# Attention and feed-forward layer on one core: spread from 32 rows, scores in three fp32r passes, GpSimd's output sums moved

## The chip, the cores and the metric

One core of one Trainium2 chip. The metric is the device time of the one launch, in microseconds. Three runs of the kernel before gave 348.83, 346.28 and 348.46; the median is 348.46.

## The reference

The input is x (4 rows of 1024 positions, 256 values), a context of 64 positions per row, and an integer mask over the context. LN is layer normalisation without weights.

```python
def attention(q_in, ctx, mask):               # 16 heads of 16; k and v have one head, shared
    q, k, v = q_in @ Wq + bq, ctx @ Wk + bk, ctx @ Wv + bv
    scores = einsum('bhqd,bkd->bhqk', q, k) / 4
    p = softmax(where(mask == 0, -1e9, scores))
    return einsum('bhqk,bkd->bhqd', p, v) @ Wo + bo

def ffn(x):                                   # 9 paths 256 -> 64 -> 256; one path for each position
    xm = mix[0] * left(x) + mix[1] * x + mix[2] * right(x)
    path = argmax(tanh(xm @ Wo1 + bo1) @ Wo2 + bo2)
    return LN(x + ((xm @ W1[path] + b1[path]) @ W2[path] + b2[path])) * gamma + beta

x = x + attention(LN(x), ctx, mask)
x = x + ffn(LN(x))
```

## The kernel before

**Chunks and steps.** Work is cut into 8 chunks of 512 positions: chunk (b, j) is half j of row b. A chunk has NT = 4 tiles of 128 positions; the model width 256 is KD = 2 blocks. Each engine (TensorE, ACT, VectorE, GpSimd, and SP for DMAs) has its own program, written out by hand, and semaphores join them. All five go through the same steps. A step has a chunk n in attention (softmax, P V, projection, LN 2), the next one, `front`, whose q and maxima are made, the one after, `after`, whose LN 1 is done, and an earlier one, f, in the FFN. For n = (r, 0) the FFN works on f = (r-1, 0), for n = (r, 1) on (r-1, 1). Steps: (0,0) and (0,1) without an FFN part, (1,0) to (3,0) full, (3,1) without a `front`, then a tail with the FFN of (3,0) and (3,1). The step shown in most rows, from 191.34 us, has n = (2,1), front (3,0), f (1,1).

**Precision.** Most large products are made in fp32r, with each operand split into a rounded high part and a remainder (hi, lo): hi*hi, hi*lo, lo*hi are three passes into one PSUM bank. W1, W2 and Wq are done so. The scores for the softmax are plain fp32, which the trace shows as two records for each matmul.

**Softmax.** `scores_for_max` makes approximate scores (position on the partitions) from the rounded q (`qr`) and the keys `kmx`; VectorE's `take_max` reduces them, and the maxima, split in two bf16 parts and transposed, are subtracted inside PSUM. `scores_transposed(t)` makes the real scores with the keys on the partitions: for each of four row quarters g of q a product of 32 rows of `kst` with 32 rows of q into bank 2+g (L556), then the mask (L559) and the maxima (L563). There are two calls, t = 0 and 1, in each step. ACT does the exponential, `pv` makes P V into banks 0 and 1 (L575) and the denominators (L581).

**Normalising the attention.** `invert` on VectorE takes the reciprocals of the denominators (L1169) and splits them in a rounded part and a remainder in different rows (L1172, L1174). `spread` on TensorE (L589) copies them to all rows with 8 products of `bc` (128 rows, ones where row and column belong together) and `rDs` into banks 4 and 5. ACT copies P V to `osb` (L872), VectorE multiplies the two (`attn_normalise`, L1180), TensorE projects with Wo (`project_out`, L599) into banks 0 and 1.

**FFN.** PSUM banks 6 and 7 are given in turn to the uses in the order of the list `uses`: h0, h4, h1, gate, h2, h3, rep0, rep1, ... `w1(m)` makes a hidden block, `gate` the path scores, VectorE's `argmax` (L1246 to L1263) turns them to a one-hot `oh`, `rep(m)` (L663) spreads it over the hidden rows, `select(m)` (L1270) keeps the chosen path, ACT rounds (`selected_hi`, L928), GpSimd makes the remainder (`selected_lo`, L1511), `w2_tiles` (L681, L682, L686) multiplies, VectorE adds the residual and applies LN 3.

**Mixing.** `second_mix` and `early_mix` on VectorE (L1207, L1209, L1212; two halves c = 0, 1) make the neighbour sum of a later FFN chunk, ACT rounds it, GpSimd makes the remainders (L1487, L1493).

**GpSimd's order in a step before.** Key operands `kmx`, `kst` (for a new row), `rstd1`, mix remainders, `value_operand` (`vd`, waits for the denominators), `add_beta` (L1480), `add_bo` (L1474), five `selected_lo`, `rstd2` (L1454, then L1467, for LN 2, which ACT applies at L892, after which TensorE transposes xh2 at L608), `rstd` of LN 3, and `finish` (L1500: times gamma; L1505: plus the residual with beta). `finish` waits for LN 3, so it runs at the beginning of the next step. SP loads the next x when `add_bo` has read the old one.

## Time and profile before

| what | value |
| --- | --- |
| median of 3 runs | 348.46 us (346.28 to 348.83) |
| profiled execution | 348.3 us, span 346.5 us |
| TensorE (PE) busy | 311.3 us, 90% of the span |
| VectorE (DVE) busy | 287.4 us, 83% |
| GpSimd (POOL) busy | 189.4 us, 55% |
| ACT busy | 177.5 us, 51% |
| mean granted clock of TensorE | 0.983 |

The span is the time from the first to the last instruction of the profiled execution; 1.8 us of its time lie around it. In the rows a number after x counts instructions that were merged into one line, the second column is the time from the first one's start to the last one's end. The shape before `f32<-` is what is written, the one behind it what is read; `128*64` before a matmul's shapes is rows and columns of the array that it uses. An fp32 matmul has two records. PEclk 1.00 means 2.4 GHz.

### The profile page before, as it was taken

The numbers are of one execution on the slowest core, as the hardware profiler recorded it, in microseconds if no ns is written. First come the engines' busy times: TensorE is split into PE (matmuls) and PEld (weight loads), VectorE is DVE, ScalarE is ACT, GpSimd is POOL, SyncE is SP. The second block draws the span as 40 slices with busy tenths as digits, with TensorE's granted clock in tenths as the row PEclk, the third lists the DMA queues.
The fourth block names the chain that finished last, engine by engine and source line by source line (L and its number), as shares of the span: only waits on it lengthen the run. The fifth ranks groups of instructions, "written<-read, shape, count | busy, mean of one in ns | idle before, by whom it ended". The sixth has DMA issues, their size and how long they took to land.

```text
span 346.5 us, 6989 instructions
## 1 busy us (share of the span) xinstructions
PE 311.3 (90%) x2700; PEld 230.7 (67%) x2700; DVE 287.4 (83%) x616; ACT 177.5 (51%) x275; POOL 189.4 (55%) x226
## 2 busy tenths in 40 slices
PE   1688889789999999999999999999999999799980
PEld 1573464556679657876779577966787578667980
DVE  2776898998789898989898998988797967689866
ACT  1354725626743676268644784377425753267400
POOL 0263202671584399628882699528962976173043
PEclk9999899999999999999999999999999999899997
DMA  7852200020020010200120010001000010001003
GB/s 225 239 117 72 78 0 3 0 77 3 2 78 0 2 61 2 78 1 8 58 76 2 1 62 2 0 3 51 11 2 1 3 62 0 0 2 61 3 0 121
DMA packets 20570, 13.53 MB, mean 39 GB/s; under 512 B 10097, under 2 KB 20282, under 8 KB 20538
## 3 DMA queue, kind: packets, MB, share of 16 engines
q1 hardware_dynamic: 18898, 12.53, 12.2%
q10 hardware_dynamic: 1640, 0.57, 0.7%
q8 instruction: 21, 0.34, 0.4%
q14 instruction: 11, 0.09, 0.1%
HBM read 8.90 MB, written 4.19 MB: 38 GB/s over the span
## 4 chain that ended last, share of the span: by engine, by line
PE 76%; DVE 14%; ACT 4%; issue 2%; DMA 2%; POOL 1%; DVEq 0%; SPq 0%; ACTq 0%; POOLq 0%
PE ps L433 16%; PE ps L438 7%; PE ps L599 7%; PE ps L681 6%; PE ps L686 5%; PE ps L682 5%; PE ps L556 5%; PE ps L581 4%; PE ps L575 4%; DVE osb L1180 3%; PE ps L663 2%; PE ps L648 2%; PE ps L559 2%; PE ps L492 2%; DVE st L1103 2%
## 5 line engine op out<-in xcount | busy, mean ns | idle before, releaser
L1454 POOL TENSOR_TENSOR rs<-ve,halfneg 128x4 f32<-128x4 f32 x24 | 26.9, 1120 | 98.0 <-DVE ve L1119 98.0
L867 ACT ACTIVATE e<-ps 128x1024 f32<-128x1024 f32 x32 | 31.1, 1024 | 16.6 <-PE ps L563 16.6
L1156 DVE TENSOR_REDUCE mx<-ps 128x16 f32<-128x1024 f32 x32 | 38.0, 1214 | 0.3 <-PE ps L531 0.3
L681 PE MATMUL ps<-w2h,hmh 128*128 128x256 f32 (+1 forms) x140 | 35.6, 289 | 0.0
L682 PE MATMUL ps<-w2l,hmh 128*128 128x256 f32 (+1 forms) x140 | 34.7, 283 | 0.0
L1511 POOL TENSOR_TENSOR hml<-hs,hmh 128x512 fp32r<-128x512 f32 x24 | 30.2, 1272 | 7.8 <-ACT hmh L928 7.7
L599 PE MATMUL ps<-wo,osb 128*128 128x256 f32 x128 | 31.3, 390 | 2.0 <-DVE osb L1180 2.0
L1500 POOL TENSOR_TENSOR y<-xh2f,gms 128x256 f32<-128x256 f32 x28 | 22.2, 824 | 17.4 <-DVE xh2f L1128 17.4
L918 ACT ACTIVATE hs<-ps,b1s 128x512 f32<-128x512 f32 x28 | 19.3, 690 | 22.6 <-PE ps L438 22.5
L433 PE MATMUL ps<-xmh,w1h 128*128 128x512 f32 x80 | 27.7, 428 | 3.0 <-DVE xmh L1231 2.2
L892 ACT ACTIVATE xh<-x,vb,rs 128x256 f32<-128x256 f32 x24 | 12.5, 591 | 32.4 <-POOL vb L1467 32.4
L928 ACT ACTIVATE hmh<-hs 128x512 fp32r<-128x512 f32 x28 | 17.4, 627 | 20.2 <-DVE hs L1270 20.2
L599 PEld LDWEIGHTS ps<-wo,osb 128*128 128x128 f32 x128 | 23.2, 190 | 6.3 <-issue 2.5
L681 PEld LDWEIGHTS ps<-w2h,hmh 128*128 128x128 f32 (+1 forms) x140 | 26.5, 189 | 0.8
L682 PEld LDWEIGHTS ps<-w2l,hmh 128*128 128x128 f32 (+1 forms) x140 | 26.4, 189 | 0.0
L438 PE MATMUL ps<-xml,w1h 128*128 128x512 f32 x80 | 26.0, 407 | 0.0
L433 PE MATMUL ps<-xmh,w1l 128*128 128x512 f32 x80 | 25.6, 401 | 0.0
L1505 POOL TENSOR_TENSOR y<-y,x1b 128x256 f32<-128x256 f32 x28 | 24.4, 899 | 0.6
L1270 DVE TENSOR_TENSOR hs<-hs,ps 128x512 f32<-128x512 f32 x28 | 18.5, 680 | 7.3 <-PE ps L663 7.3
L1474 POOL TENSOR_TENSOR x<-xin,bos 128x256 f32<-128x256 f32 x32 | 23.9, 778 | 0.8
L686 PE MATMUL ps<-w2h,hml 128*128 128x256 f32 (+1 forms) x140 | 21.4, 282 | 0.3 <-POOL hml L1511 0.3
L556 PE MATMUL ps<-q,kst 32*128 32x512 f32 x128 | 19.1, 640 | 1.2 <-ACT e L867 1.2
(163 smaller groups left out, 791.8 us busy)
## 6 DMA issues: line engine op xcount, KB each, us to landing
xin<-in_x SPq DMA_DIRECT2D x8, 512.0 KB, 3.7
out<-y SPq DMA_DIRECT2D x7, 512.0 KB, 2.9
min_<-in_mask_Bx1xSxS_ik SPq DMA_DIRECT2D x8, 128.0 KB, 4.2
hs<-in_L_ffn_W SPq DMA_DIRECT2D x2, 288.0 KB
y<-in_constants SPq DMA_DIRECT2D x1, 512.0 KB, 10.1
hs<-in_L_ffn_W SPq DMA_DIRECT2D x1, 512.0 KB
out<-xin SPq DMA_DIRECT2D x2, 256.0 KB, 2.2
cst<-in_constants SPq DMA_DIRECT2D x1, 384.0 KB, 6.7
```

The source lines that it names most:

```text
L433: nc.tensor.matmul(out_, lhs[i](k), rhs(k), start=(i == 0 and k == 0), stop=False)
L438: mm = nc.tensor.matmul(out_, lhs(k), rhs(k), start=False, stop=(k == KD - 1))
L556: nc.tensor.matmul(ps[:, 2 + g, :], kst[quarter(g), :], q[quarter(g), t, :], start=True, stop=False)
L599: mm = nc.tensor.matmul(ps[:, k // 2, (k % 2) * D:(k % 2 + 1) * D], osb[:, c, k * P:(k + 1) * P], wo[:, c, :], start=(c == 0), stop=(c == ...
L681: nc.tensor.matmul(o, L.hi(m, r)[:, ks], w2h[0:r, m, :], start=(m == 0), stop=False)
L682: nc.tensor.matmul(o, L.hi(m, r)[:, ks], w2l[0:r, m, :], start=False, stop=False)
L686: mm = nc.tensor.matmul(o, L.lo(m, r)[:, ks], w2h[0:r, m, :], start=False, stop=(m == NM - 1))
L867: nc.scalar.activation(e[:, 2 * i:2 * i + 2, :], ps[:, bank:bank + 2, :], ACT.Exp).then_inc(s_e, 1)
L1156: v.tensor_reduce(mx[:, k, :].rearrange("p (a h) -> p a h", a=2), ps[:, bank:bank + 2, :].rearrange("p a (h s) -> p a h s", s=SK), AX.X, A ...
L1454: g.tensor_tensor(ln[7][:, :], ln[6][:, :], halfneg[:, :], ALU.pow).then_inc(s_r, 1)
L1505: a = g.tensor_tensor(y[:, k], y[:, k], x1b[:, j, k], ALU.add)
L1511: g.tensor_tensor(usual.lo(m, r), usual.selected(m, r), usual.hi(m, r).bitcast(F32), ALU.subtract).then_inc(s_hl, 1)
```

## The change

- **Spread.** The constant `bc` holds for each 32 rows what it held for 128: KD * P columns instead of KD * NT * P. `spread` takes for tile k only the 32 rows (row quarter k) that hold its reciprocals, and writes bank `SPREAD_BANKS[k]` = 0, 1, 4, 5. So it waits for the P V copy as well. `attn_normalise` is two instructions of two tiles each, and `project_out` waits for its own half.
- **First mask behind P V.** rep(0), the first block of the path mask, is made by TensorE right behind `pv`, ahead of w1(2) and w1(3); the order of the two banks changes with it. VectorE's `select(0)` stands ahead of `invert`. The tail keeps the old order by a class of its own (`behind`).
- **Scores.** ACT's q copy writes the rounded q (`qr`) itself. VectorE's `q_lo` makes the remainder from PSUM, bias and `qr`, in place of the cast; it stands between the two halves of the mixes. The banks of q are free only after it. GpSimd makes `ksth` and `kstl` beside `kst`. `scores_transposed` makes 12 fp32r products (three passes over the four quarters) instead of 4 fp32 ones.
- **GpSimd's order.** `finish` of a chunk stands one step later, behind the mix remainders (and `value_operand`), ahead of `selected_lo`; then `add_beta`, in full steps `rstd2`, and then `add_bo`. LN 3 writes to `y`, so `xh2f` is free sooner, and VectorE waits there for the store of the chunk before.
- **Argmax.** Its scores and candidates stay in the gate's PSUM bank instead of SBUF tiles.
- `wk8` and the loaded copy of `bc` lie in other tiles. The load of the spread constants is a quarter of its size.

```diff
             def spread(b, j):
                 pe.wait_ge(s_rd, at(b, NJ, j + 1))
+                pe.wait_ge(s_osb, at(b, NJ, j + 1))
                 for c in range(KD):
                     for k in range(NT):
-                        mm = nc.tensor.matmul(ps[:, 4 + c, k * P:(k + 1) * P], bc[:, c, k, :], rDs[:, :],
-                                              start=True, stop=True)
+                        mm = nc.tensor.matmul(ps[:, SPREAD_BANKS[k], c * P:(c + 1) * P], bc[quarter(k), c, :],
+                                              rDs[quarter(k), :], start=True, stop=True)
                 mm.then_inc(s_bc, 1)
             def project_out(b, j, tiles):
-                if tiles[0] == 0:
-                    pe.wait_ge(s_osb, at(b, NJ, j + 1))
-                    pe.wait_ge(s_oT, at(b, NJ, j + 1))
+                pe.wait_ge(s_oT, at(b, 2 * NJ, 2 * j + tiles[0] // 2 + 1))
...
                 for g in range(4):
                     if t and g % 2 == 0:
                         pe.wait_ge(s_e, at(b, NJ * 4, j * 4 + g // 2 + 1))
-                    nc.tensor.matmul(ps[:, 2 + g, :], kst[quarter(g), :], q[quarter(g), t, :], start=True, stop=False)
+                    nc.tensor.matmul(ps[:, 2 + g, :], ksth[quarter(g), :], qr[quarter(g), t, :], start=True, stop=False)
+                for g in range(4):
+                    nc.tensor.matmul(ps[:, 2 + g, :], kstl[quarter(g), :], qr[quarter(g), t, :], start=False, stop=False)
+                for g in range(4):
+                    nc.tensor.matmul(ps[:, 2 + g, :], ksth[quarter(g), :], ql[quarter(g), t, :], start=False, stop=False)
...
# pv: waits for q_lo instead of the q copy
-                    pe.wait_ge(s_q, at(b, NJ * KD, (j + 2) * KD))
+                    pe.wait_ge(s_ql, at(b, NJ * KD, (j + 2) * KD))
...
# TensorE, step; uses = ["h0", "h4", "h1", "gate", "rep0", "h2", "h3", "rep1", ...]
                 if f:
+                    rep(*f, 0)
                     w1(*f, 2)
                     w1(*f, 3)
-                    rep(*f, 0)
...
# VectorE
-            def q_round(b, j):
+            def q_lo(b, j, bank):
...
                 for m in range(KD):
-                    dve.wait_ge(s_q, at(b, NJ * KD, j * KD + m + 1))
-                    a = v.tensor_copy(qr[:, m, :], q[:, m, :])
-                a.then_inc(s_qr, 1)
+                    dve.wait_ge(s_qr, at(b, NJ * KD, j * KD + m + 1))
+                    v.scalar_tensor_tensor(out=ql[:, m, :], in0=ps[:, bank + m, :], scalar=bqs[:, m:m + 1],
+                                           in1=qr[:, m, :].bitcast(F32), op0=ALU.add, op1=ALU.subtract).then_inc(s_ql, 1)
...
             def attn_normalise(b, j):
...
-                v.tensor_tensor(osb[:, :, :], osb[:, :, :], ps[:, 4:6, :], ALU.mult).then_inc(s_oT, 1)
+                for half in range(2):
+                    h, banks = slice(2 * half * P, 2 * (half + 1) * P), slice(SPREAD_BANKS[2 * half], SPREAD_BANKS[2 * half] + 2)
+                    o = osb[:, :, h].rearrange("p c (k t) -> p k c t", k=2)
+                    v.tensor_tensor(o, o, ps[:, banks, 0:KD * P].rearrange("p k (c t) -> p k c t", c=KD),
+                                    ALU.mult).then_inc(s_oT, 1)
...
# VectorE, step
                 if f and f[1] == 0:
-                    second_mix(f[0])
+                    second_mix(f[0], (0,))
                 if f and n[1] == NJ - 1:
-                    early_mix(n[0])
+                    early_mix(n[0], (0,))
                 if front:
-                    q_round(*front)
+                    q_lo(*front, 0 if f else 6)
+                if f and f[1] == 0:
+                    second_mix(f[0], (1,))
+                if f and n[1] == NJ - 1:
+                    early_mix(n[0], (1,))
...
                 if f:
                     argmax(*f)
+                    select(*f, 0)
                 if n:
                     invert(*n)
-                if f:
-                    select(*f, 0)
...
             def layernorm3_apply(b, j):
                 c = at(b, NJ, j + 1)
-                normalise(lambda k: xh2f[:, k, :], lambda k: xh2f[:, k, :], ln3, s_ln3r, s_ln3, c)
+                dve.wait_ge(s_out[1 - j], at(b, 16, 16))
+                normalise(lambda k: y[:, k, :], lambda k: xh2f[:, k, :], ln3, s_ln3r, s_ln3, c)
...
# GpSimd, step (before = the chunk in front of f)
+                if before:
+                    finish(*before)
+                if f:
+                    for m in range(NM):
+                        selected_lo(*f, m)
                 if next_f:
                     add_beta(*next_f)
+                if n and front and f:
+                    rstd2(*n)
                 if front:
...
                     add_bo(*front, next_f)
-                if f:
-                    for m in range(NM):
-                        selected_lo(*f, m)
-                if n:
+                if n and not (front and f):
                     rstd2(*n)
                 if f:
                     rstd(ln3, s_ln3v, s_ln3r, at(f[0], NJ, f[1] + 1))
-                if f:
-                    finish(*f)
```

## Rows read from the trace of the kernel before

**Rows 1.** The page, part 4: the chain that ended last, by engine.

```profile
PE 76%; DVE 14%; ACT 4%; issue 2%; DMA 2%; POOL 1%; DVEq 0%; SPq 0%; ACTq 0%; POOLq 0%
```

**Rows 2.** Busy time by stretch, one step; (x) is the number of instructions.

```profile
191.00:229.00 38.00, 37.75 (x338) 28.13 (x336) 34.35 (x72) 22.74 (x37) 27.19 (x32) 1.00 0.04 15
```

**Rows 3.** TensorE in order of time, step (0,1): start, length, what; in brackets its wait.

```profile
69.40 3.69 PE L599 MATMUL ps<-wo,osb 128*128 128x256 f32 x16 [0.59 <-DVE osb L1180]
```

**Rows 4.** TensorE in order of time, the step that begins at 191.34, first half and its end.

```profile
191.34 1.14 PE L556 MATMUL ps<-q,kst 32*128 32x512 f32 x8
...
192.41 0.60 PE L559 MATMUL ps<-mT,cst 64*128 64x512 bf16 x4
...
192.95 0.40 PE L563 MATMUL ps<-nmT,cst 32*128 32x512 bf16 x4
...
193.27 0.74 PE L433 MATMUL ps<-xmh,w1h 128*128 128x512 f32 x2
...
194.78 0.62 PE L433 MATMUL ps<-xmh,w1h 128*128 128x512 f32 x2
195.24 0.63 PE L433 MATMUL ps<-xmh,w1l 128*128 128x512 f32 x2
...
207.14 0.73 PE L433 MATMUL ps<-xmh,w1h 128*128 128x512 f32 x2
...
226.63 1.04 PE L608 MATMUL ps<-cst,xh 128*128 128x128 f32 x8
```

**Rows 5.** TensorE in order of time, same step, around the spread.

```profile
210.49 1.11 PE L589 MATMUL ps<-rDs,bc 128*128 128x128 f32 x8
211.52 0.41 PE L663 MATMUL ps<-cst,oh 128*64 128x128 bf16 x8
211.87 0.39 PE L527 MATMUL ps<-cst,mT 64*128 64x512 bf16 x2
...
212.43 0.41 PE L663 MATMUL ps<-cst,oh 128*64 128x128 bf16 x8
```

**Rows 6.** VectorE in order of time, same step.

```profile
198.26 0.96 DVE L1207 TENSOR_SCALAR xm<-x2T,mks 128x511 f32<-128x511 f32 x1
...
203.96 0.76 DVE L1150 CAST qr<-q 128x512 fp32r<-128x512 f32 x2
...
209.19 0.74 DVE L1174 SCALAR_TENSOR_TENSOR rDs<-rDs,cst,rD 128x128 fp32r<-128x128 f32 x1
...
211.63 1.22 DVE L1180 TENSOR_TENSOR osb<-osb,ps 128x1024 f32<-128x1024 f32 x1 [0.28 <-PE ps L589]
```

**Rows 7.** ACT in order of time, same step.

```profile
201.27 0.69 ACT L855 ACTIVATE q<-ps,bqs 128x512 f32<-128x512 f32 x1 [0.21 <-PE ps L438]
...
206.85 1.01 ACT L872 ACTIVATE osb<-ps 128x1024 f32<-128x1024 f32 x1
...
223.78 2.08 ACT L892 ACTIVATE xh<-x,vb,rs 128x256 f32<-128x256 f32 x4 [5.61 <-POOL vb L1467]
```

**Rows 8.** One line each: duration ns min/median/max, first and last start.

```profile
L1257 DVE TENSOR_TENSOR cand<-gs,gmax x8: 197/907/1178, 90.9 to 319.4; 128x36 f32<-128x36 f32 x8
...
L1259 DVE TENSOR_TENSOR gs<-cand,cst x8: 197/1203/1211, 92.1 to 319.7; 128x36 f32<-128x36 f32 x8
```

**Rows 9.** GpSimd in order of time, same step.

```profile
194.42 2.82 POOL L1500 TENSOR_TENSOR y<-xh2f,gms 128x256 f32<-128x256 f32 x4 [2.19 <-DVE xh2f L1128]
197.32 3.64 POOL L1505 TENSOR_TENSOR y<-y,x1b 128x256 f32<-128x256 f32 x4
...
204.73 2.52 POOL L1493 TENSOR_TENSOR xml<-xm,xmh 128x511 fp32r<-128x511 f32 x2
...
207.63 2.90 POOL L1480 TENSOR_TENSOR x1b<-x,bts 128x256 f32<-128x256 f32 x4
...
218.87 1.29 POOL L1511 TENSOR_TENSOR hml<-h4s,hmh 73x512 fp32r<-73x512 f32 x1
...
222.30 1.02 POOL L1454 TENSOR_TENSOR rs<-ve,halfneg 128x4 f32<-128x4 f32 x1 [2.14 <-DVE ve L1119]
```

More of the change, by code:

```diff
@@ L319, in x @@
                 return xh2f[:, k, :]
+        class BehindSteps(Usual):
+            uses = ["h0", "h4", "h1", "gate", "h2", "h3", "rep0", "rep1", "rep2", "rep3", "rep4", "w2a", "w2b"]
+            by_act = [u in ("h4", "h0", "h1", "h2", "h3") for u in uses]
         class Last(Path):
@@ L786, in _ @@
             f0, f1 = (B - 1, 0), (B - 1, 1)
-            w1(*f0, 0)
-            w1(*f0, 4)
-            w1(*f0, 1)
-            gate(*f0)
-            w1(*f0, 2)
-            w1(*f0, 3)
-            rep(*f0, 0)
-            rep(*f0, 1)
+            w1(*f0, 0, behind)
+            w1(*f0, 4, behind)
+            w1(*f0, 1, behind)
+            gate(*f0, behind)
+            w1(*f0, 2, behind)
+            w1(*f0, 3, behind)
+            rep(*f0, 0, behind)
+            rep(*f0, 1, behind)
             w1(*f1, 4, last)
-            rep(*f0, 2)
+            rep(*f0, 2, behind)
             w1(*f1, 0, last)
-            rep(*f0, 3)
+            rep(*f0, 3, behind)
             w1(*f1, 1, last)
-            rep(*f0, 4)
+            rep(*f0, 4, behind)
             gate(*f1, last)
@@ L805, in _ @@
                 rep(*f1, m, last)
-            w2_tiles(*f0, range(NT))
+            w2_tiles(*f0, range(NT), behind)
             w2_tiles(*f1, range(NT), last)
@@ L908, in hidden @@
                 bank = L.bank(j, f"h{m}")
-                if L is usual and m == 0:
+                if L is not last and m == 0:
                     act.wait_ge(s_hl, 1 + at(b, NJ * NM, j * NM))
@@ L1193, in x1_stats, with mix @@
                     variance(ln2, (s_ln2s, s_ln2h, s_ln2p, s_ln2v), c, 2 * c, -1.0)
-            def mix(b, j, last, sems):
+            def mix(b, j, last, sems, parts):
                 dve.wait_ge(s_x2T, at(b, NJ * KD, (j + 1) * KD))
-                for c in range(KD):
+                for c in parts:
                     n = at(b, KD, c + 1)
@@ L1280, in residual @@
                 c = at(b, NJ, j + 1)
-                if half == 0 and L is usual:
+                if half == 0 and L is not last:
                     dve.wait_ge(s_xh2f, c)
@@ L1285, in residual @@
                 k = 2 * half
-                x = xh2f[:, k:k + 2, :] if L is usual else xh2[:, 1, k:k + 2, :]
+                x = xh2f[:, k:k + 2, :] if L is not last else xh2[:, 1, k:k + 2, :]
                 v.tensor_tensor(x, x, ps[:, L.bank(j, use), :].rearrange("p (k d) -> p k d", d=D), ALU.add).then_inc(L.s_fv, 1)
@@ L1321, in step @@
                     argmax(*f)
+                    select(*f, 0)
                 if n:
                     invert(*n)
-                if f:
-                    select(*f, 0)
-                elif front:
+                if front and not f:
                     take_max(*front, 0, banks)
@@ L1392, in _ @@
             dve.wait_ge(s_lones, 1)
-            argmax(*f0)
+            argmax(*f0, behind)
             mixed_lo(*f1)
-            select(*f0, 0)
-            select(*f0, 1)
-            selected_lo(*f0, 0)
-            select(*f0, 2)
-            selected_lo(*f0, 1)
-            select(*f0, 3)
-            selected_lo(*f0, 2)
-            select(*f0, 4)
-            selected_lo(*f0, 3)
-            selected_lo(*f0, 4)
+            select(*f0, 0, behind)
+            select(*f0, 1, behind)
+            selected_lo(*f0, 0, behind)
+            select(*f0, 2, behind)
+            selected_lo(*f0, 1, behind)
+            select(*f0, 3, behind)
+            selected_lo(*f0, 2, behind)
+            select(*f0, 4, behind)
+            selected_lo(*f0, 3, behind)
+            selected_lo(*f0, 4, behind)
             argmax(*f1, last)
@@ L1511, in selected_lo, with step @@
                 g.tensor_tensor(usual.lo(m, r), usual.selected(m, r), usual.hi(m, r).bitcast(F32), ALU.subtract).then_inc(s_hl, 1)
-            def step(n, front, f, after, next_f):
+            def step(n, front, f, after, next_f, before=None):
                 if front and front[1] == 0:
@@ L1555, in _ @@
             for r in range(1, B - 1):
[L1556 to L1559 removed]
+                step((r, 0), (r, 1), (r - 1, 0), (r + 1, 0), (r - 1, 1), (r - 2, 1) if r > 1 else None)
+                step((r, 1), (r + 1, 0), (r - 1, 1), (r + 1, 1), (r, 0), (r - 1, 0))
+            step((B - 1, 0), (B - 1, 1), (B - 2, 0), None, (B - 2, 1), (B - 3, 1))
+            step((B - 1, 1), None, (B - 2, 1), None, (B - 1, 0), (B - 2, 0))
             f0, f1 = (B - 1, 0), (B - 1, 1)
+            finish(B - 2, 1)
             for k in range(NT):
```

124 lines of the change are left out of this document (61 added, 63 removed).

## The prediction

> **What bounds the kernel now.** I read the chain that ended last first, then the busy time of each engine by stretch, then one whole step engine by engine. The chain lies 76% on TensorE, 14% on VectorE and 1% on GpSimd [rows 1]. In the step from 191 to 229 us TensorE is busy 37.75 of 38.00 us, VectorE 34.35, ACT 22.74, GpSimd 27.19 [rows 2]. So from chunk (1,0) to (3,0) a microsecond taken from TensorE is a microsecond of time, unless another engine then comes late; a cut on VectorE or GpSimd is worth nothing by itself. In the two steps before that, and in step (3,1), which carry less FFN work, TensorE waits for VectorE, for instance 0.59 us for the normalised attention output [rows 3]. The profiled execution took 348.3 us for a span of 346.5; I sum against 348.3, and the median of the runs, 348.46, is no different.
>
> All times below are those of the step that begins at 191.34 (n = (2,1)), unless said.
>
> **Scores for the softmax (16 calls).** Now four fp32 products of 32 rows and 512 columns take 191.34 to 192.41, 1.07 us from start to start [rows 4]. The change makes twelve fp32r products, three on each row quarter. A single pass over four quarters exists in bf16: 192.95 to 193.27, 0.32 us with the change of tile shape behind it [rows 4]. A further fp32r pass of 512 columns costs 0.46 us for two, 0.23 each, in W1's stream (194.78 to 195.24) [rows 4]. That four fp32r quarters run beside each other is not in the trace; two halves do: two bf16 products of 512 columns and four fp32r ones of 256 fit into 211.87 to 212.43, 0.56 us, where one after the other they would need 4 x 0.23 = 0.92 [rows 5]. I take 0.32 + 2 x 0.23 = 0.78, a saving of 0.29 a call and 4.6 us in all. Bounds: three full passes of 0.32 save 0.11 a call (1.8 us); no overlap at all, 12 x 0.23 = 2.8 us, would lose 27 us, which the overlap of the halves speaks against. The row shows 4 x 0.23 / 0.32 = 2.9 times the speed of one after the other. The Trainium skill (TensorE: Matmul & The Clock Gate, Measured speedup vs the span model) gives 3.07 for four row tiles of K = 32, N = 512, not 4; if every pass had only that, a pass would be 0.30 and the saving 0.17 a call, 2.7 us in all. The row agrees with it for one pass; whether the loss comes once or with each pass no row says.
>
> **Spread (8 calls).** Eight fp32r products of 128 rows, 210.49 to 211.52, 1.03 us [rows 5]. They become eight products of 32 rows, two on each quarter, into four banks. Nearest row: rep, eight bf16 products of 128 columns on half the array's columns, 0.35 us from 211.52 to 211.87 [rows 5]. I take 0.40, saving 0.63; bounds 0.35 and 1.03 (no overlap, nothing saved).
>
> **Normalisation.** One VectorE instruction of 1.22 us [rows 6] becomes two of about 0.65. Where TensorE waits for it ((0,1) and (3,1)) the projection starts 0.57 earlier. In a full step it isn't the projection that waits but the second scores-for-max, whose banks 4 and 5 the second half still frees: behind the spread lie 212.43 - 211.52 = 0.91 us plus one rep, 1.26 us, and VectorE needs 0.1 + 1.3. That costs about 0.15 us a step, where the present one is about 0.1.
>
> **New waits of the spread.** It writes banks 0 and 1, so ACT's copy of P V must be done: 207.86 [rows 7], hidden by W1. It also stands behind select(0) now. P V and denominators end at 207.14 - 0.58 = 206.6; rep 0 ends at 206.95, select(0) (0.69, half of 1.22 and a start cost) at 207.65; the inversion, which ends at 209.19 + 0.74 = 209.93 now and takes 2.2 us, ends at 209.9 again. TensorE comes to the spread at 206.6 + 0.35 + 3.0 (two w1: 210.49 - 0.35 - 207.14) = 209.95. No wait, and no reserve: I take 0.1.
>
> **rep 0 ahead of two w1** needs the one-hot by 206.6. VectorE's two mix halves take 5.70 us, 198.26 to 203.96 [rows 6], 2.85 each. Between them now stands q_lo, which replaces the two casts and waits for ACT's second q copy: 201.96 - 0.29 x 2 = 201.4 [rows 7], plus 0.65 = 202.05; second mix half until 204.9 at most. The argmax is six small instructions. Two of them, on SBUF, take 907 and 1203 ns in the median and 197 at best [rows 8]. At 0.2 each with their gaps the six take 1.4 us: 206.3, in time. P V's wait for q_lo (banks 0, 1) is over at 202.05, and P V can't come before 202.1: the q products are over at 200.7 then (ACT's copy of 0.69 ends at 201.4), and a w1 of 6 x 0.23 and the gate scores lie between. Covered. The long ones are those that run beside GpSimd. The Trainium skill (SBUF — State Buffer, Who interferes with whom) says that a VectorE instruction with at most one SBUF input and outside the two-port modes doesn't contend; by it the PSUM versions stay at 0.2. If they kept their present medians instead, the one-hot would come 1.7 us later, at 208.0, and rep 0 would wait 1.4 us in every full step: no gain at all.
>
> **GpSimd.** finish (8 instructions, 2.82 + 3.64 and a gap, 6.5 us [rows 9]) leaves the head of the step, where it holds up mixes and operands, and stands behind the mix remainders and ahead of selected_lo. kst needs two instructions more in every second step; hidden at the head. In the step shown the second mix half ends at 204.9 at most; one of ACT's copies and half of the 2.52 us of the remainders [rows 9] put GpSimd at about 206.8, vd follows the denominators, and finish ends at 213.4, five selected_lo of 1.28 (the last starts at 218.87 now [rows 9]) at 219.8. TensorE comes to them 0.95 earlier than now, and now W2 doesn't wait for the last, which ends at 220.16: so at worst 219.8 - 219.2 = 0.6 us of wait, most likely none, and I take none. Then add_beta, 2.90 [rows 9], which stood at 207.63 before: 222.7. rstd2, which began at 222.30, starts 0.4 later though its input comes 0.9 earlier. From there to ACT's start 1.48 us and 2.08 for the apply [rows 7, 9]: 226.3. The transposes of xh2, now at 226.63 [rows 4], want to start at 225.7. **New wait: 0.5 us** in the odd steps. In the even ones GpSimd builds no operands beside the mixes and no vd ahead of finish; I take finish 0.5 us earlier there (an estimate: vd's wait for the denominators and the held-up mixes), and the wait as near nothing. add_bo, and with it the next load of x, ends near 227.1; now it follows add_beta at 210.53 and, at the same length, ends at 213.4: the load is due on VectorE about 3 us behind the next step's start at 229, some 5 us later, and VectorE then has slack ahead of q_lo, so I cost it at nothing; that cover gone, a microsecond of lateness is a microsecond of time. The smaller load of constants and the halved cast at the start lie beside other work: nothing.
>
> **The sum.** A full step gains 2 x 0.29 + 0.63 on TensorE, less 0.15 and 0.1: about 0.95. Even steps (1,0), (2,0), (3,0): 2.8. Odd ones (1,1), (2,1), less 0.5: 0.9. (0,0): VectorE sets the order behind the denominators, so only the scores: 0.6. (0,1): scores 0.6 and 0.5 by the first half: 1.1. (3,1): 0.6 + 0.6 + 0.5, less 0.6 for GpSimd's later remainders: 1.1. The tail after 299 us has neither part. Total 6.5 us: 348.3 - 6.5 = 341.8.
>
> **Rivals.**
> 1. Nothing else comes late: GpSimd's finish loses its contention with the mixes and LN2 is in time everywhere. Then 4.6 + 6 x 0.63 + 1.0 = 9.4 us: 339. For it: the reserve at the transposes is missed by only 0.5 us. Against: no reserve at four places at once. 0.2.
> 2. The quarters overlap poorly (scores save 0.11 to 0.17 a call, spread 0.3): 2.3 + 2.4 - 1 = 3.7 us: 344.6. For it: one pass has 0.32 where the stream has 0.23. 0.18.
> 3. Slower: GpSimd's row of work takes TensorE's place. Everything between the mix remainders and rstd2 now runs as one string of 16 us; each microsecond by which it begins or runs later goes straight into the five full steps through LN2 and the transposes. At 1.3 us of lateness per step the whole gain is gone, from there it is slower; at 2 us it costs 10 us and gives 352. For it: finish's instructions have been held up by VectorE (0.91 us each in the second half against 0.70 in the first). Against: VectorE works from PSUM in most of that stretch. 0.12.
> 4. The new orders and the gains cancel within a microsecond or two (one-hot or inversion late by a microsecond): 347. 0.1.
> The forecast, 341.8, has 0.4.
>
> **Numbers.** A change below 1% (3.5 us) can't be told from none here: the three runs spread over 0.7%. Faster by over 1% (below 345): the forecast, rival 1, and half of rival 2: 0.7. Within 1%: 0.19. Slower: 0.11. Range 338 to 348.5: it takes in rivals 1, 2 and 4; left out is rival 3 and a more complete gain.
>
> **What the changed profile would show.** The scores line near 0.8 us for twelve records, start to start (right), above 1.0 (rival 2); spread near 0.4; the two argmax instructions near 0.2 us; TensorE without a wait at rep 0; a wait of the xh2 transposes for ACT's LN2 apply, released by GpSimd, larger in odd steps; step period 36.8 to 37.3 instead of 37.7. Waits of over 1 us at rep 0, at the spread or at the transposes would make the forecast wrong, and so would a wait of VectorE for x.

## The result, and the profile after

The changed kernel took 350.92 us in the median of 4 runs (350.37 to 352.21) where the kernel before took 348.35 in the same job: a ratio of 1.0098, with a 95% interval of 1.0061 to 1.0134. It is slower, and 9 us above the forecast of 341.8. The profiled execution took 350.6 us for a span of 348.8.

The chain that ended last lay 76% on TensorE [rows 1]. In the changed kernel:

```profile
PE 39%; DVE 38%; issue 9%; ACT 8%; POOL 3%; DMA 1%; DVEq 0%; SPq 0%; POOLq 0%; ACTq 0%
```

Busy time by stretch, the steps (2,0) and (2,1); the columns are length, busy time of TensorE's products, of its weight loads, VectorE, ACT, GpSimd with their counts, granted clock, and DMA (share and GB/s):

```profile
152.81:191.19 38.38, 36.78 (x342) 27.73 (x343) 34.08 (x76) 22.31 (x36) 23.98 (x28) 1.00 0.10 32
191.19:229.98 38.79, 36.80 (x343) 27.75 (x343) 33.97 (x72) 22.33 (x36) 26.49 (x33) 1.00 0.10 32
```

The stretch of [rows 2] was cut at round figures. Between the transposes of layer norm 1, with which TensorE begins each step, the period before was 37.73 us, of which TensorE was busy 37.48. TensorE's work fell by 0.7 us, and yet the period grew by 1.06 in (2,1) and 0.65 in (2,0). So the work was saved and waits took its place. TensorE in order of time through (2,1) shows both; its step is 0.85 us later here than in the rows of before:

```profile
192.19 0.51 PE L561 MATMUL ps<-qr,ksth 32*128 32x512 f32 x4
192.52 0.40 PE L563 MATMUL ps<-qr,kstl 32*128 32x512 f32 x4
192.75 0.41 PE L565 MATMUL ps<-ql,ksth 32*128 32x512 f32 x4
193.09 0.61 PE L568 MATMUL ps<-mT,cst 64*128 64x512 bf16 x4
...
208.49 0.41 PE L672 MATMUL ps<-cst,oh 128*64 128x128 bf16 x8 [0.77 <-DVE oh L1280]
...
212.29 0.44 PE L600 MATMUL ps<-rDs,bc 32*128 32x128 f32 x8 [0.39 <-DVE rDs L1185]
212.67 0.41 PE L672 MATMUL ps<-cst,oh 128*64 128x128 bf16 x8
...
228.51 0.74 PE L617 MATMUL ps<-cst,xh 128*128 128x128 f32 x5 [0.50 <-ACT xh L901]
```

The scores take 193.09 - 192.19 = 0.90 us in place of 1.07 [rows 4]; the spread 212.67 - 212.29 = 0.38 in place of 1.03 [rows 5]. Three waits are new: for the one-hot ahead of rep 0, for the inversion ahead of the spread, for layer norm 2 ahead of the transposes, 1.66 us together. Over the kernel the table of waits gives them 3.1, 1.3 and 3.0 us. VectorE in the same step:

```profile
198.89 0.75 DVE L1227 SCALAR_TENSOR_TENSOR xm<-x2T,mks,xm 128x511 f32<-128x511 f32 x1
201.59 0.75 DVE L1161 SCALAR_TENSOR_TENSOR ql<-ps,bqs,qr 128x512 fp32r<-128x512 f32 x1 [1.95 <-ACT qr L864]
202.50 0.75 DVE L1161 SCALAR_TENSOR_TENSOR ql<-ps,bqs,qr 128x512 fp32r<-128x512 f32 x1 [0.15 <-ACT qr L864]
203.16 0.48 DVE L1222 TENSOR_SCALAR xm<-x2T,mks 128x511 f32<-128x511 f32 x1
...
204.46 1.81 DVE L1227 SCALAR_TENSOR_TENSOR xm<-x2T,mks,xm 128x511 f32<-128x511 f32 x1
206.20 0.19 DVE L1264 TENSOR_TENSOR ps<-ps,bo2s 128x36 f32<-128x36 f32 x1
...
207.13 0.20 DVE L1278 TENSOR_REDUCE gidx<-ps 128x4 f32<-128x36 f32 x1
207.36 0.98 DVE L1280 TENSOR_TENSOR oh<-cst,gidx 128x36 bf16<-128x36 f32 x1
209.01 0.69 DVE L1287 TENSOR_TENSOR hs<-hs,ps 128x512 f32<-128x512 f32 x1 [0.67 <-PE ps L672]
209.62 0.95 DVE L1180 RECIPROCAL rD<-ps 128x128 f32<-128x128 f32 x1
210.60 0.76 DVE L1183 CAST rDs<-rD 128x128 fp32r<-128x128 f32 x1
211.40 0.84 DVE L1185 SCALAR_TENSOR_TENSOR rDs<-rDs,cst,rD 128x128 fp32r<-128x128 f32 x1
...
222.65 0.86 DVE L1120 TENSOR_TENSOR su<-st 128x12 f32<-128x12 f32 x1
223.43 0.77 DVE L1121 TENSOR_TENSOR dm<-st 128x4 f32<-128x4 f32 x1
```

The second mix half stands behind q's remainders, for which VectorE waits 1.95 us. Its last instruction takes 1.81 us where its fellow of the first half took 0.75, and the one-hot takes 0.98 where the argmax in PSUM takes 0.20. The inversion (L1180 to L1185) takes 209.62 to 212.24, 2.62 us, where it took 2.24 before. GpSimd shows what lies beside them:

```profile
204.45 1.28 POOL L1518 TENSOR_TENSOR xml<-xm,xmh 128x511 fp32r<-128x511 f32 x1 [1.58 <-ACT xmh L913]
207.02 1.27 POOL L1518 TENSOR_TENSOR xml<-xm,xmh 128x511 fp32r<-128x511 f32 x1 [1.29 <-ACT xmh L913]
...
208.46 2.82 POOL L1524 TENSOR_TENSOR y<-y,gms 128x256 f32<-128x256 f32 x4
211.36 2.84 POOL L1529 TENSOR_TENSOR y<-y,x1b 128x256 f32<-128x256 f32 x4
...
221.35 2.83 POOL L1505 TENSOR_TENSOR x1b<-x,bts 128x256 f32<-128x256 f32 x4
224.81 1.02 POOL L1479 TENSOR_TENSOR rs<-ve,halfneg 128x4 f32<-128x4 f32 x1 [0.64 <-DVE ve L1128]
```

The remainder of mix half 1 runs from 204.45 to 205.73, over the 1.81 us instruction, and that of half 2 from 207.02 to 208.29, over the one-hot. The output sums (208.46 to 214.20) lie over the whole inversion. x1 plus beta runs from 221.35 to 224.18 over VectorE's two variance instructions (0.86 and 0.77; 0.17 and 0.16 where nothing runs beside them), which then let GpSimd itself wait 0.64 us for the variance.

### The profile page after: what moved, and what is told of

It is laid out like the page before. It is cut to its first block, busy times and chain, and to the rows that moved or that the text cites. A ratio compares the mean times of both kernels' runs of the same rounds, so it can differ in the third digit from the quotient of the medians.

```text
span 348.8 us, 7135 instructions
## 1 busy us (share of the span) xinstructions
PE 303.2 (87%) x2764; PEld 228.8 (66%) x2764; DVE 287.2 (82%) x624; ACT 177.4 (51%) x275; POOL 183.7 (53%) x234
## 4 chain that ended last, share of the span: by engine, by line
PE 39%; DVE 38%; issue 9%; ACT 8%; POOL 3%; DMA 1%; DVEq 0%; SPq 0%; POOLq 0%; ACTq 0%
PE ps L439 11%; DVE mx L1167 7%; PE ps L444 5%; DVE st L1112 4%; ACT xh L901 3%; DVE x L1203 3%; DVE xm L1227 3%; DVE su L1120 2%; PE ps L497 2%; DVE osb L1194 2%; POOL rs L1479 2%; PE ps L568 2%; DVE hs L1287 2%; DVE rD L1180 2%; PE ps L561 2%
## 5 line engine op out<-in xcount | busy, mean ns | idle before, releaser
L1479 POOL TENSOR_TENSOR rs<-ve,halfneg 128x4 f32<-128x4 f32 x24 | 25.2, 1051 | 72.9 <-DVE ve L1128 72.8
L1499 POOL TENSOR_TENSOR x<-xin,bos 128x256 f32<-128x256 f32 x32 | 24.8, 804 | 0.1
L1524 POOL TENSOR_TENSOR y<-y,gms 128x256 f32<-128x256 f32 x28 | 19.7, 737 | 7.6 <-DVE y L1137 7.6
L1512 POOL TENSOR_TENSOR xml<-xm,xmh 128x512 fp32r<-128x512 f32 x6 | 7.6, 1279 | 26.6 <-ACT xmh L908 26.6
L1529 POOL TENSOR_TENSOR y<-y,x1b 128x256 f32<-128x256 f32 x28 | 20.7, 770 | 0.5
```

The costliest lines, as they stand in the source:

```text
L1479: g.tensor_tensor(ln[7][:, :], ln[6][:, :], halfneg[:, :], ALU.pow).then_inc(s_r, 1)
L1499: a = g.tensor_tensor(x1[:, j, k], xin[:, j, k], bos[:, :], ALU.add)
```

## The experiments

Times are medians in us; the ratio is to the kernel before, run in the same job, with its 95% interval. The kernel before took 348.35 us beside the changed kernel, 347.61 beside e1 to e4, 347.47 beside e5 to e8 and 347.31 beside e9 to e12. The changed kernel was run only in the first of these jobs, so a difference in us between it and an experiment is uncertain by one to two us. By the ratios, e1, e2, e9 and e11 lie 3.4, 3.4, 3.1 and 6.1 us below it. The last columns are TensorE's period in three full steps, between the first rows of layer norm 1's transposes.

| kernel | us | ratio | (1,1) | (2,0) | (2,1) |
|---|---|---|---|---|---|
| before | 348.35 | | 37.74 | 37.73 | 37.73 |
| changed | 350.92 | 1.0098 (1.0061 to 1.0134) | 38.79 | 38.38 | 38.79 |
| e1 q's remainders later | 347.45 | 1.0000 (0.9979 to 1.0020) | 37.66 | 37.29 | 37.66 |
| e2 root first | 347.24 | 1.0000 (0.9979 to 1.0021) | 38.36 | 37.91 | 38.12 |
| e3 both | 348.28 | 1.0016 (0.9992 to 1.0041) | 38.71 | 37.28 | 38.30 |
| e4 GpSimd's old order | 345.47 | 0.9948 (0.9930 to 0.9967) | 36.94 | 38.42 | 36.90 |
| e5 e4, first mask in old place | 342.92 | 0.9877 (0.9837 to 0.9916) | 37.09 | 37.36 | 37.08 |
| e6 e4, q's remainders later | 354.12 | 1.0189 (1.0133 to 1.0245) | 42.16 | 38.71 | 41.01 |
| e7 e5 with two passes | 343.73 | 0.9909 (0.9874 to 0.9945) | 36.92 | 37.38 | 36.92 |
| e8 output sums in old place | 347.94 | 1.0026 (0.9991 to 1.0060) | 37.49 | 38.83 | 37.44 |
| e9 first mask in old place | 347.66 | 1.0009 (0.9987 to 1.0032) | 37.78 | 37.79 | 37.80 |
| e10 e5, normalise first | 349.08 | 1.0075 (1.0050 to 1.0101) | 37.75 | 38.02 | 37.74 |
| e11 e2 and e9 | 344.11 | 0.9922 (0.9894 to 0.9950) | 37.09 | 37.10 | 37.09 |
| e12 before, spread alone | 345.34 | 0.9957 (0.9926 to 0.9987) | 37.44 | 37.43 | 37.43 |

**e1: q's remainders behind both mix halves.**

```diff
-                    second_mix(f[0], (0,))
-                if front:
-                    q_lo(*front, 0 if f else 6)
-                    second_mix(f[0], (1,))
+                    second_mix(f[0])
+                if front:
+                    q_lo(*front, 0 if f else 6)
```

> The changed kernel (350.9 us) with one edit on VectorE: q's two remainders are issued behind both halves of the mix instead of between them. Theory A (the queue order on VectorE is the loss): in the changed kernel VectorE stands idle 1.95 us for ScalarE's second q tile with the second mix half queued behind it, so the one-hot ends at 208.3 in step (2,1) and rep 0 waits 0.77 us, the spread 0.39 us. Here the second mix half fills the idle time, q's remainders still end at about 203.3, the six steps of the argmax run right behind the gate, rep 0 and the spread wait under 0.1 us, and five full steps win 1.1 to 1.2 us each: 345 us. Theory B (GpSimd's output sums, contending with VectorE, are the loss, and the queue order only shows it): waits move by less than 0.3 us a step, 349.5 to 351 us.

The waits of rep 0 and the spread went (the table of waits has none for the one-hot, and one of 0.2 us for the spread), and the full steps became 1.1 us shorter, as theory A had it. The time fell by 3.5 us, not the 5.8 expected; the layer norm 2 wait grew from 3.0 to 3.4 us in all.

**e2: the reciprocal root for layer norm 2 ahead of x1 plus beta.**

```diff
+                if n and f:
+                    rstd2(*n)
                 if next_f:
                     add_beta(*next_f)
-                if n and front and f:
-                    rstd2(*n)
...
-                if n and not (front and f):
+                if n and not f:
                     rstd2(*n)
```

> The changed kernel with one edit on GpSimd: the reciprocal root for layer norm 2 is issued ahead of x1 plus beta in every step with an FFN path, the last one included. Theory A (x1 plus beta holds VectorE's tiny variance instructions and then GpSimd itself): the two instructions that took 0.86 and 0.77 us (2.66 us in the last step) fall to 0.2 us, the wait of the second transposes for layer norm 2 goes (0.50 us in (2,1), 1.17 us in the last step), the waits for the one-hot and the spread stay: about 2.5 us less than the changed kernel, 348.4 us. Theory B (VectorE's chain before that is late by itself): the wait stays, 350 to 351 us.

GpSimd in (2,1), which begins 1.12 us earlier here than in the changed kernel:

```profile
222.42 1.02 POOL L1479 TENSOR_TENSOR rs<-ve,halfneg 128x4 f32<-128x4 f32 x1 [2.14 <-DVE ve L1128]
223.52 0.34 POOL L1492 TENSOR_TENSOR vb<-mu,rs 128x4 f32<-128x4 f32 x1
223.82 3.01 POOL L1505 TENSOR_TENSOR x1b<-x,bts 128x256 f32<-128x256 f32 x4
```

The two variance instructions took 0.17 and 0.16 us, and TensorE no longer waits for layer norm 2. The time fell by 3.7 us, where 2.5 was expected; the even steps had such a wait too (0.29 us in (2,0), whose period is 0.47 us shorter here). The difference from 2.5 us is within the noise between jobs.

**e3: both.** 

> Both edits together: q's remainders behind both mix halves, and the reciprocal root for layer norm 2 ahead of x1 plus beta. If the two losses are separate (theory A of both): 350.9 - 5.8 - 2.5 = 342.6 us, against a forecast of 341.8 us for the change. If one late chain feeds both: no better than the better of the two single edits, 345 us.

The two gains don't add: 348.28 us, no better than either edit alone (the 1 us between them is within the intervals), and 3 us above what one late chain was said to give. A new wait stands in their place. TensorE first, then VectorE, in (2,1):

```profile
203.56 1.92 PE L584 MATMUL ps<-e,vd 128*32 128x512 f32 x16 [1.27 <-issue]
```

```profile
194.77 1.40 DVE L1112 BATCH_NORM_STATS2 st<-xin 128x6 f32<-128x256 f32 x4 [1.02 <-DMA xin<-in_x]
...
202.05 1.40 DVE L1161 SCALAR_TENSOR_TENSOR ql<-ps,bqs,qr 128x512 fp32r<-128x512 f32 x2
203.37 0.20 DVE L1264 TENSOR_TENSOR ps<-ps,bo2s 128x36 f32<-128x36 f32 x1
```

With the root first, x plus bo, which reads the buffer that the load of x fills, ends 1.6 us after the step's start instead of 0.8 before it, and VectorE waits 1.02 us for that load. With q's remainders last, this lateness goes on into them: they end at 203.45, and P V, which may not write its banks before they are read, starts at 203.56. "issue" at the end of a wait only says that the trace names no releaser; `pv` has a wait for q's remainders, and the last one ends 0.11 us earlier. In (1,1) the same wait is 1.67 us.

**e4: GpSimd's step in the order of before.**

```diff
-                if before:
-                    finish(*before)
-                if f:
-                    for m in range(NM):
-                        selected_lo(*f, m)
                 if next_f:
                     add_beta(*next_f)
-                if n and front and f:
-                    rstd2(*n)
...
                     add_bo(*front, next_f)
-                if n and not (front and f):
+                if f:
+                    for m in range(NM):
+                        selected_lo(*f, m)
+                if n:
                     rstd2(*n)
...
+                if f:
+                    finish(*f)
```

> The changed kernel with GpSimd's step in the order of the kernel before (x1 plus beta, x plus bo, selected remainders, reciprocal roots, then the output sums of the same step), all else as changed. Theory A (VectorE's order holds rep 0 and the spread; GpSimd's order only the second transposes): the 0.50 us of layer norm 2 go, the one-hot stays late; 1.5 to 2.5 us less than the changed kernel, 348.5 to 349.5 us. Theory B (the output sums behind the mix remainders are the whole loss): all three waits go, 343 us. Theory C (in their old place the sums collide with layer norm 1 and the mix of the next step, as in the kernel before): 351 us or more.

Between A and B: 5.4 us less than the changed kernel. The odd steps have none of the three waits (36.9 us), the even one has all of the one-hot's:

```profile
168.68 0.41 PE L672 MATMUL ps<-cst,oh 128*64 128x128 bf16 x8 [1.24 <-DVE oh L1280]
```

In the odd steps the operands of the next row delay GpSimd's mix remainders until VectorE's second mix half is over; in the even ones there are none, and the remainder lies over the last mix instruction (1.65 us).

**e5: e4 with the first mask in its old place** (the edit of e9, on top of e4). 

> The kernel with GpSimd's old order (345.5 us) and, besides, the first mask back in its old place: rep 0 behind the last two products of w1 on TensorE, its selection behind the inversion on VectorE. There the step (2,0) took 38.42 us, with a wait of 1.24 us for the one-hot ahead of rep 0 and 0.23 us for the spread; the step (2,1), in which the one-hot was in time, took 36.90 us. Theory A (the early place of rep 0 only exposes the one-hot, and nothing else needs it early): the 1.4 us of w1 2 and 3 cover the one-hot, both steps take 36.9 us, (2,0) and (3,0) win 1.2 to 1.5 us each: 343 us. Theory B (the inversion is now behind a late one-hot and the spread takes over the wait): the wait of the spread grows by 1 us in (2,0), 345 to 346 us.

The time is that of theory A, 342.92 us; the steps are not quite, 37.36 and 37.08 us where it had 36.9 for both. This version beats both kernels. TensorE keeps waits of 0.3 to 0.4 us a step for the normalisation, and 0.2 for rep 0 in (2,0).

**e6: e4 with e1's edit.** 

> The kernel with GpSimd's old order (345.5 us) and, besides, q's remainders behind both mix halves. Theory A (P V waits for q's remainders, and behind a mix that the output sums hold they come late): in (2,1) they end at about 204 us of that kernel's clock where P V wants them at 202.3, a new wait of about 1.5 us ahead of P V in the odd steps, nothing won there, 1.2 us won in the even ones: 345.5 to 347 us. Theory B (the remainders have slack behind the mix): all full steps at 36.9 to 37.3 us, 343 us.

The direction of theory A, but far more than it gave: the wait ahead of P V is 2.3 us in both odd steps, and 354.12 us. One of the six runs took 989 us, and nothing on record says why; the other five took 352.69 to 357.01. In (2,0), where theory A had 1.2 us won, the wait is 1.84 us and nothing is won. The stretches before, in and behind the wait in (2,1); the figure behind the five engines is the granted clock:

```profile
200.00:208.30 8.30, 8.30 (x52) 5.70 (x50) 8.09 (x15) 6.48 (x10) 8.22 (x11) 1.00 0.16 57
208.30:210.60 2.30, 0.09 (x1) 0.00 (x0) 2.27 (x5) 0.98 (x2) 2.17 (x3) 1.00 0.08 25
210.60:214.20 3.60, 3.53 (x21) 1.20 (x25) 1.33 (x6) 2.08 (x4) 2.65 (x3) 0.53 0.02 5
214.20:217.00 2.80, 2.80 (x79) 2.42 (x71) 0.50 (x1) 1.02 (x1) 0.77 (x2) 1.00 0.00 0
```

**e7: e5 with one pass of the scores left out** (it leaves out the product of the keys' remainder and the rounded q).

```diff
-                for g in range(4):
-                    nc.tensor.matmul(ps[:, 2 + g, :], kstl[quarter(g), :], qr[quarter(g), t, :], start=False, stop=False)
```

> As the kernel with GpSimd's old order and the first mask in its old place, with one of the three passes of the scores left out (the keys' remainder by q rounded; so the scores lack that term). In the trace of the changed kernel the three passes start 0.33, 0.23 and 0.34 us apart, 0.90 us a call. Theory A (the middle pass costs what its 4 x 512 columns take at full overlap and the rest is a price of changing the shape of the tile, paid once at either end): 0.23 us less a call, 16 calls, 3.7 us less. Theory B (each pass pays 0.30 us): 0.30 us a call, 4.8 us less. If VectorE or ScalarE paces a step by now, less than 2 us.

A call now takes 0.68 us from start to start (189.97 to 190.65), 0.22 less: theory A's size for a pass. But the steps fell by at most 0.17 us and not by 2 x 0.22, since P V now comes up against q's remainders (a wait of 0.36 us in (2,0)); the time didn't fall (0.9909 against e5's 0.9877, with overlapping intervals). In this execution TensorE's clock was also lower before the steps begin, 0.6 in one slice.

**e8: only the output sums in their old place.**

```diff
-                if before:
-                    finish(*before)
...
+                if f:
+                    finish(*f)
```

> The changed kernel (350.9 us) with only the output sums back at the end of GpSimd's step; the selected remainders, x1 plus beta, the reciprocal root and x plus bo stay in the changed order. In the trace of the changed kernel the sums (2 x 2.84 us) push the selected remainders from 214.2 and x1 plus beta to 221.4 to 224.2, onto VectorE's variance. Theory A (the place of the sums is what makes GpSimd's string late): x1 plus beta ends before the variance, layer norm 2 is in time, casts of the inversion are not held: 345.5 us, as with the whole old order. Theory B (the order of the rest matters as much: x plus bo behind it all lets the load of x come late): 347 to 349 us, with a wait of VectorE for the load of x.

The time is theory B's, 347.94 us, but not by its reason: VectorE doesn't wait for the load of x in any full step. The wait for layer norm 2 stays (3.6 us in all), so the place of the sums is not what holds the variance. In (2,0) the one-hot is late as in e4 (1.28 us); in the odd steps rep 0 waits no more. The wait of the spread is gone too: without the sums beside it the inversion takes 1.60 us in every step (in (2,1) its last two instructions take 0.23 and 0.35 us in place of 0.76 and 0.84).

**e9: the changed kernel with the first mask in its old place.**

```diff
-                    rep(*f, 0)
                     w1(*f, 2)
                     w1(*f, 3)
+                    rep(*f, 0)
...
-                    select(*f, 0)
                 if n:
                     invert(*n)
+                if f:
+                    select(*f, 0)
```

> The changed kernel (350.9 us) with one edit: the first mask back in its old place (rep 0 behind w1 2 and 3 on TensorE, its selection behind the inversion on VectorE). The one-hot comes 0.8 us late there in (2,1) and the spread 0.4 us. Theory A (w1 2 and 3, 1.4 us, cover the one-hot; the inversion, which needs only P V, goes a mask's product earlier): both waits go, the wait for layer norm 2 (0.5 us in odd steps) stays, 1.0 to 1.2 us a full step less: 345.5 us. Theory B (the inversion starts behind the late one-hot all the same, and the spread wants it 0.35 us later than now at most): the spread waits 0.5 us or more, 348 us.

Both waits went, and the full steps fell to 37.8 us (by 1.0 in the odd ones, 0.6 in (2,0)), as in theory A. The time fell by 3.3 us; I had expected 5.4. The transposes still waited for layer norm 2, and the scores-for-max behind the spread for the normalisation. In (2,1):

```profile
212.75 0.39 PE L532 MATMUL ps<-cst,mT 64*128 64x512 bf16 x2 [0.31 <-DVE osb L1194]
...
227.15 1.06 PE L617 MATMUL ps<-cst,xh 128*128 128x128 f32 x8 [0.52 <-ACT xh L901]
```

**e10: e5 with the normalisation ahead of the first selection.** 

> The best kernel so far (342.9 us) with one edit on VectorE: P V's normalisation ahead of the first selection. Its trace shows TensorE waiting 0.30 us in (2,1) and 0.43 us in (2,0) for the first half of the normalisation, behind the selection of rep 0 (0.69 us). Theory A: that wait goes, 0.3 to 0.4 us a full step: 341.3 us. Theory B (rep 2 then waits for the selection, which reads the bank that it needs, and the selected tiles come later on ScalarE and GpSimd): 342.9 us or more.

Theory B: 6 us worse than e5. The wait of 0.30 us is gone, and rep 2 waits for the selection, which reads its bank:

```profile
212.78 0.41 PE L672 MATMUL ps<-cst,oh 128*64 128x128 bf16 x8 [0.96 <-DVE hs L1287]
```

**e11: e2's and e9's edits together, the output sums left where the change puts them.** 

> The changed kernel with two edits: the reciprocal root for layer norm 2 ahead of x1 plus beta, and the first mask in its old place; the output sums stay behind the mix remainders. Theory A (the new place of the sums costs nothing by itself once the two waits that it feeds are gone): full steps at 37.0 to 37.4 us, 343 to 344 us, level with the kernel that has GpSimd's old order. Theory B (with the sums there, x plus bo ends so late that the load of x reaches VectorE about 1 us late, and the mix and the one-hot move with it): 1 us more in each full step, 346 us or more.

Theory A: 344.11 us, and 37.1 us in each of the three full steps. From the changed kernel, e2 takes 3.7 us, e9 3.3 and both together 6.8 (3.4, 3.1 and 6.1 by the ratios): within the noise these are two separate losses that add. In (2,1), TensorE, then VectorE, then GpSimd:

```profile
207.79 0.41 PE L672 MATMUL ps<-cst,oh 128*64 128x128 bf16 x8
208.13 0.44 PE L600 MATMUL ps<-rDs,bc 32*128 32x128 f32 x8
...
210.25 0.39 PE L532 MATMUL ps<-cst,mT 64*128 64x512 bf16 x2 [0.30 <-DVE osb L1194]
...
223.97 1.04 PE L617 MATMUL ps<-cst,xh 128*128 128x128 f32 x8
```

```profile
193.62 1.41 DVE L1112 BATCH_NORM_STATS2 st<-xin 128x6 f32<-128x256 f32 x4 [0.91 <-DMA xin<-in_x]
...
204.28 0.20 DVE L1278 TENSOR_REDUCE gidx<-ps 128x4 f32<-128x36 f32 x1
204.50 1.00 DVE L1280 TENSOR_TENSOR oh<-cst,gidx 128x36 bf16<-128x36 f32 x1
```

```profile
204.16 1.28 POOL L1519 TENSOR_TENSOR xml<-xm,xmh 128x511 fp32r<-128x511 f32 x1 [1.29 <-ACT xmh L913]
```

The load of x is late here too (0.91 us), and the one-hot still takes 1.00 us beside GpSimd's remainder. Neither is waited for: w1 2 and 3 lie ahead of rep 0, and q's remainders ahead of the second mix half.

**e12: the kernel before with the new spread alone.** 

> The kernel before (347.5 us on this chip) with the new spread and the two halves of the normalisation alone. In the changed kernel the spread took 0.38 us in place of 1.03. Theory A (all of it on TensorE's path): 8 x 0.65 = 5.2 us less, 342.3 us. Theory B (the spread now waits for the inversion or for ScalarE's copy of P V, or the first output product for the normalisation, in the steps with an FFN path): half of it is given back, 345 us.

Theory B: 345.34 us, 2.0 less. TensorE's busy time in a step falls by 0.59 us, to 36.89, but the period only by 0.30: the second scores-for-max now waits 0.30 us for the normalisation, where it waited 0.07 before.

```profile
212.84 0.39 PE L527 MATMUL ps<-cst,mT 64*128 64x512 bf16 x2 [0.30 <-DVE osb L1182]
```

It waits for the second half, which frees banks 4 and 5 and ends at 212.78 (the first ends at 212.18). The expectation of e10 calls the same wait one for the first half.

## Why the prediction was wrong, by its own steps

**Scores.** The lower bound of its own rows came nearer than the value taken: 0.90 us and not 0.78, a saving of 0.17 a call, 2.7 us in all and not 4.6. The three passes start 0.33, 0.23 and 0.34 us apart. So the middle pass has the price of the stream and the loss comes twice, at both ends, which is what the step had left open. The estimate from the Trainium skill (TensorE: Matmul & The Clock Gate, Measured speedup vs the span model), 0.17 a call, was exact in its sum, though not by 0.30 for each pass: one pass left out gave 0.22 (e7).

**Spread.** Right: 0.38 us for 0.40. TensorE's busy time in a full step fell from 37.48 to 36.55 in e11, 0.93, against 1.21 taken and 2 x 0.17 + 0.65 = 0.99 measured at the two places.

**Normalisation.** The wait priced at 0.15 us is 0.15 in four of the five full steps of the changed kernel, but 0.30 where no other wait covers it (e11, e12). In (0,1) the 0.5 us expected didn't come: that period grew from 24.11 to 24.67. The projection no longer waits 0.59 us, but TensorE then waits 0.88 us for the split maxima, where it waited 0.20. They come at the end of VectorE's own string, which from the reciprocals on takes 9.0 us here and before, so halving the normalisation shortened nothing. The step had looked only at the wait for the normalisation. The new spread alone (e12), without a change on GpSimd, gives the same 0.80 us of wait and the same 24.66. Some 0.4 of the 0.56 us of growth lies ahead of P V, and is not taken apart here; the period differs by up to 0.9 us between the traces.

**The step that failed: rep 0 ahead of two w1, "in time".** On the prediction's clock the second mix half was to end at 204.9 at most and the one-hot at 206.3; shifted by the 0.85 us of this trace, 205.75 and 207.15. They ended at 206.27 and 208.34, 0.52 and 1.19 us late. The mix half began 0.26 us late, behind q's remainders, and took 3.11 us for the 2.85 priced. 2.85 was the length before, which had some contention with GpSimd in it; without any, the three instructions take 2.1 us (201.75 to 203.88 in e4). The argmax then took 2.07 us for 1.4. Its five instructions in PSUM were right to the figure (0.20 each); the sixth, the one-hot, has both inputs in SBUF and took 0.98. The text knew which instructions GpSimd can hold, and yet priced all six at 0.2. Both long instructions, the last of the mix (1.81 for 0.75) and the one-hot, lie beside GpSimd's mix remainders. The change itself put them there: by splitting the mix around q's remainders it makes the remainder of the first half due while the second half runs. e4 has both cases in one trace: in (2,1) that remainder starts behind the mix, whose last instruction takes 0.75 us, and rep 0 doesn't wait; in (2,0) it lies beside the remainder and takes 1.65 us, and rep 0 waits 1.24. In the changed kernel rep 0 waited 0.77 us for the one-hot in (2,1).

The spread's "no reserve" failed for a reason of its own. Both TensorE's two w1 and VectorE's selection start from rep 0, so a late rep 0 moves both and opens no gap between them. What opened it is the inversion, priced at 2.2 us and measured 2.62 in (1,1) and (2,1) and 2.42 in (2,0) and (3,0), beside the output sums that the change had moved there; the spread waits 0.39 and 0.19 us. In (1,0), where no sums run, the inversion takes 1.60 and the spread doesn't wait, and the same holds for every step of e8. e9, which moves the first mask back on both engines, ends both waits and makes the full steps 0.6 to 1.0 us shorter. The range held back 0.1 for this case (rival 4), and didn't add it to anything else.

**GpSimd.** The wait foreseen in odd steps was 0.5 us and measured 0.50, but the cause was half missed. finish ended at 214.2, selected_lo at 221.4, add_beta at 224.2, all 0.8 to 1.6 us later than said, 0.85 of it the shift. I let rstd2 wait for add_beta alone; add_beta in its turn held VectorE's variance, so that rstd2 began 0.64 us later still. "Near nothing" in even steps was wrong: the wait is 0.29 us there, and e2 takes 0.47 us off (2,0). W2 did not wait for the selected remainders in the full steps, as said; in (3,1) it waited 0.84 us (0.31 before), where the sum had 0.6.

**The load of x at nothing.** Right for the changed kernel; e3 and e11 show the cover and its end: at 1 us of lateness it is free with q's remainders between the mix halves and costs 1.27 us ahead of P V with them behind.

**Rivals.** What came is neither of them alone. Rival 4 (one-hot or inversion late, 347) and rival 3's mechanism (GpSimd's string into layer norm 2) came together, with 0.5 us a step from the second where the rival had 2. I had them as alternatives; e2, e9 and e11 (3.7, 3.3, 6.8 us) show that they add. The new place of the output sums is no harm by itself: e11, with the sums there, takes 37.1 us a step, as e5 does in its odd steps with them in the old place. In the changed kernel it isn't free either: moving only the sums back (e8) takes 3.0 us off (2.5 by the ratio), by the inversion and by rep 0 in the odd steps.

**The size of the gain.** Without the two losses the change is faster, but the sum of 6.5 us doesn't stand. e11 is 3.2 us faster than the kernel before it in its job, e5 4.5, and a full step gains 0.64 us for the 0.95 taken. Of the 9.1 us between forecast and result, 6 to 7 are the two losses. The rest fits gain that the sum had and no run shows: 1.9 us of the scores, some 0.15 us a full step of the normalisation, and the 1.1 us of (0,1), which grew instead.

**What stays open.** e9's three full steps explain some 2.6 us of its 3.3. How its earlier steps trade with each other ((0,1) 0.9 shorter, (1,0) 0.5 longer) I have not taken apart. e5 and e11 were run in different jobs, and their intervals overlap, so which of them is faster isn't settled.

## What to carry to other kernels

When an instruction moves to a place without reserve, list what the other engines run in those microseconds, and price it at its length beside them, not at its best. Ask of each wait what starts both of its sides: a late start that they share opens no gap between them. Losses at different places of a step can add up (e11), so two rivals of 0.1 each are also a joint case; two edits that each remove one need not (e3). And move a step back alone before condemning the whole change: here two places in the order cost 6 to 7 us, and hid a gain of 0.8%.

## What the runs showed of the hardware

- In full steps, stalls ahead of P V of 1.27 and 1.67 us (e3) and of 1.84 us (e6, (2,0)) left TensorE's granted clock at 1.00 behind them, the 2.4 GHz level. The two of 2.3 us (e6, (1,1) and (2,1)) were followed by P V at the 1.2 GHz level, in 3.64 and 3.62 us in place of 1.92. So those stalls cost about twice their length: the odd steps grew by 5.2 and 4.1 us against e4.
- Beside GpSimd instructions on SBUF, VectorE's tiny instructions with both inputs in SBUF can be held until one of them ends: the variance's went from 0.17 and 0.16 us to 0.86 and 0.77, the one-hot from 0.20 to 0.98. The end of the running one isn't always enough. In (3,1) the first variance instruction starts at 291.94, beside a selected remainder, and takes 2.66 us, over three instructions of x1 plus beta as well. Nor are they always held: the second took 0.15 us in three of the steps. The reduction in PSUM from 207.13 on, under the same GpSimd instruction as the one-hot, stayed at 0.20 us. The Trainium skill (SBUF — State Buffer, Who interferes with whom) names the case with at most one SBUF input as free, and the rows agree.
- The profiled executions of the fourteen kernels differ outside the full steps too: the transposes with which (0,1) begins start between 49.0 and 50.9 us, and the stretch from the start of the last chunk's w1 to the end takes 45.8 us in e2, e5 and e8 and 46.6 to 47.0 in the others, by whether the clock has an 8 in slice 35 of the page. So a microsecond between two profiles can be the clock's and not the edit's. e5, and below it the changed kernel:

```profile
PEclk9999999999999999999999999999999999999996
```

```profile
PEclk9989999999999999999999999999999999899996
```
